# Second cross attention of a decoder on one core: scores in 64-row passes, three of four maxima copied and merged in one operation

## What is computed

```
x = stable_layernorm(x, g_norm)
q = x @ Wq;  k, v = split(context @ Wkv)            # 8 heads of 64
k, v = concat(null_kv, k), concat(null_kv, v)       # one key more
q = l2norm(q) * q_scale;  k = l2norm(k) * k_scale
sim = q @ k.T * 8;  sim = where(mask, sim, -max)
attn = softmax(sim, axis=-1)                        # float32
out = stable_layernorm((attn @ v) @ Wo, g_out)
```

## Time and profile before

| | before |
|---|---|
| median of 3 runs | 2707.45 us (2706.44 to 2709.51) |
| span of the profiled execution, first to last instruction | 2706.5 us |
| PE busy | 2391.5 us (88%) |
| DVE busy | 2051.9 us (76%) |
| ACT busy | 1528.1 us (56%) |
| mean granted TensorE clock, as a share of full speed | 0.929 |
| exponentials of the stage, line 2490 | 408, 433.1 us |
| adds, line 2802 | 400, 486.8 us |
| takes, line 2740 | 208, in three forms by source |
| merges, line 2751 | 192, 127.4 us |

### The profile page before, as it was taken

One profiled execution on the slowest core, in us unless ns is written; L12 is line 12 of the kernel. 1 busy time (PEld: TensorE's weight loads), 2 busy tenths in 40 slices (PEclk: granted clock), 3 DMA queues, 4 the chain that ended last, 5 costly groups with the idle time before them and its releaser, 6 DMA issues. The chain is left out here.

```text
span 2706.5 us, 33877 instructions
## 1 busy us (share of the span) xinstructions
PE 2391.5 (88%) x10276; PEld 872.1 (32%) x10276; DVE 2051.9 (76%) x3028; ACT 1528.1 (56%) x1858; POOL 302.4 (11%) x333
## 2 busy tenths in 40 slices
PE   6888677999999979998466599999999999997998
PEld 3555411222222224444122133323333333332443
DVE  5676698999995224344797888989999998976775
ACT  5555496777768843333443566666666666653111
POOL 5665500000000000000164100000000000000000
PEclk8898957999999989999698599999999999998998
DMA  5454471220001159954003331122113111111100
GB/s 142 134 166 140 132 109 35 62 66 27 26 24 29 31 111 215 212 152 117 17 0 65 77 96 30 29 64 71 30 30 105 30 30 29 31 36 69 47 0 8
DMA packets 198858, 191.06 MB, mean 71 GB/s; under 512 B 18288, under 2 KB 159125, under 8 KB 197905
## 3 DMA queue, kind: packets, MB, share of 16 engines
q1 hardware_dynamic: 198573, 189.13, 27.0%
q10 hardware_dynamic: 144, 0.10, 0.0%
HBM read 144.28 MB, written 41.42 MB: 69 GB/s over the span
## 5 line engine op out<-in xcount | busy, mean ns | idle before, releaser
L2802 DVE TENSOR_TENSOR y_acc<-y_acc,y_probs 128x1024 f32<-128x1024 f32 x400 | 486.8, 1217 | 35.1 <-ACT y_probs L2490 23.3
L2490 ACT ACTIVATE y_probs<-y_E,y_mask_bias 128x1024 f32<-128x1024 f32 x408 | 433.1, 1111 | 72.0 <-PE y_E L2582 63.9
L1223 ACT ACTIVATE x_probs<-x_E 128x1024 f32<-128x1024 f32 x408 | 396.6, 1022 | 136.2 <-PE x_E L1283 134.2
L1406 DVE TENSOR_REDUCE x_maxima<-x_M 128x1 f32<-128x496 f32 x660 | 410.5, 669 | 27.4 <-PE x_M L1265 17.1
L2591 PE MATMUL y_O<-y_probs,y_values 128*64 128x512 f32 x1632 | 400.1, 611 | 0.0
L2581 PE MATMUL y_E<-y_qa,y_ks 128*128 128x512 f16 x816 | 313.4, 384 | 1.5 <-ACT y_copied L2463 1.2
L2582 PE MATMUL y_E<-y_qb,y_ks 66*128 66x512 f16 x816 | 311.6, 382 | 0.0
L2463 ACT ACTIVATE y_copied<-y_M 128x1024 bf16<-128x1024 f32 (+1 forms) x164 | 162.4, 990 | 213.1 <-PE y_M L2545 213.1
L2740 DVE TENSOR_REDUCE y_maxima<-y_M 128x2 f32<-128x1024 f32 (+2 forms) x195 | 231.2, 1186 | 41.2 <-PE y_M L2545 31.4
L1874 DVE TENSOR_TENSOR f_hidden<-f_act_out,f_spread 128x512 f32<-128x512 f32 x160 | 110.7, 693 | 174.2 <-ACT f_act_out L1705 143.2
L1296 PE MATMUL x_O<-x_probs,x_values 128*32 128x512 f32 x1632 | 218.1, 606 | 0.4 <-ACT x_probs L1223 0.4
(11 more groups left out here) (503 smaller groups left out, 3159.1 us busy)
## 6 DMA issues: line engine op xcount, KB each, us to landing
f_spread<-comb_dram SPq DMA_DIRECT2D x160, 256.0 KB, 5.9
y_values<-v_dram SPq DMA_DIRECT2D x208, 128.0 KB, 2.2
v_dram<-a_v_out SPq DMA_DIRECT2D x26, 512.0 KB, 2.6
k_dram<-a_k_parts SPq DMA_DIRECT2D x26, 512.0 KB, 3.3
x_values<-v_dram SPq DMA_DIRECT2D x100, 128.0 KB, 2.2
f_weights<-f_w_in SPq DMA_DIRECT2D x40, 256.0 KB, 8.8
y_ks<-k_dram SPq DMA_DIRECT2D x75, 128.0 KB, 2.8
v_dram<-a_v_out SPq DMA_DIRECT2D x26, 256.0 KB, 2.1
```

The costliest lines, as they stand in the source:

```text
L1223: nc.scalar.activation(probs[:, n % 2, 2 * g:2 * g + 2, :], psE[:, 2 * g:2 * g + 2, :], ACT.Exp).then_inc(exped, 1)
L1406: V.tensor_reduce(maxima[:, 2 * h + j, qt, c:c + 1], psM[(2 * entry + j) % 3][:, 0:CHUNK0], AX.X, ALU.max).then_inc(max_done, 1)
L2490: A(probs[:, i, :], psE[:, 2 * (i % 2):2 * (i % 2) + 2, :].rearrange("p a b -> p (a b)"), ACT.Exp, bias=mask_bias[:, bass.ds(c * TILES_IN_ ...
L2802: ins = V.tensor_tensor(acc[:, u % 2, :], acc[:, u % 2, :], probs[:, i, :], ALU.add)
```

## The change

The second fp16 arrangement goes: keys and queries are no longer stacked by parts, and head j keeps rows 64 j to 64 j + 63 in one tile each (`keys`, `q_parts`). The scores of a tile are now four pairs of 64-row matmuls, the two heads of a pair side by side in the array: high on high, low on high, high on low, and a pair that adds the maxima (`m_ones` on `m_rows`). The DMAs that laid out `qa` and `qb` are gone, and the key loads take 2 DMAs instead of 5.

Of the four maxima of a chunk DVE takes only the first. ACT copies the other three, and one DVE operation merges all three (128x3072). All four maxima of the main part use `psM`, one after the other. On PE a half turn is now: a maximum, the scores of two tiles, a maximum, `weigh` of two tiles. Cut to its core:

```diff
-        copied = sb("copied", [P, 2, 2 * 512], BF16)
+        copied = sb("copied", [P, 3, 2, 512], BF16)
-        PV0, MAX0, SUM0, SPARE0, MERGED0 = 4, 2, 4, 2, 2
+        PV0, MAX0, SUM0, SPARE0, MERGED0 = 4, 2, 4, 3, 2
+        def spare_number(u, c, q):
+            return c * SPARES + (SPARES * KEY_TURNS * u + q - 1)
+        def merge_number(u, c):
+            return c + ((KEY_TURNS - 1) * u - 1)
...
# ACT
-                def copy_spare(u, c, g, scores=psM[:]):
+                def copy_spare(u, c, q, scores=psM[:]):
...
-                        e.wait_ge(S["merged"], merge_number(u, c, g) + 1)
-                        out = copied[:, g, :].rearrange("p (j n) -> p j n", j=2)
+                        e.wait_ge(S["merged"], merge_number(u, c) + MERGED0)
+                        out = copied[:, q - 1, :, :]
...
-                            if i == 1 and not (u == 0 and isinstance(c, int) and c == 0):
-                                copy_spare(*before(u, c), 1)
-                            if i == 3:
-                                copy_spare(*ahead(u, c), 0)
+                            if i == 0 and not (u == 0 and isinstance(c, int) and c == 0):
+                                copy_spare(*before(u, c), 3)
+                            if i >= 2:
+                                copy_spare(*ahead(u, c), i - 1)
# PE
+                def next_maximum(u, c, q):
+                    if q != 1:
+                        e.wait_ge(S["spare_copied"], spare_number(u, c, max(q, 1)) + SPARE0)
+                    if q < 2:
+                        e.wait_ge(S["max_done"], number(u, c) + (q + MAX0))
+                    maximum(u, c, q, psM, S["spare_mm"] if q else S["max_mm"])
...
+                    for key_part, q_part in ((0, 0), (1, 0), (0, 1)):
+                        for j in range(2):
+                            r = head_rows(j)
+                            T.matmul(psE[:, 2 * slot + j, :], keys[r, u // 2 % 2, key_part, tile * P:tile * P + P],
+                                     q_parts[r, q_part, u // 2, q0:q0 + HALF], start=(key_part + q_part == 0), stop=False)
...
+                            next_maximum(*ahead(u, c), 2 * g)
                                 for i in range(2):
                                     scores(u, c * TILES_IN_TURN + (2 * g + 2 + i), i, n + (2 + i))
-                            late_first(*ahead(u, c), g)
+                            next_maximum(*ahead(u, c), 2 * g + 1)
...
-                            late_spare(*ahead(u, c), g)
# DVE
-                    e.wait_ge(S["spare_copied"], number(u, c, g) + 1 + SPARE0)
-                    e.wait_ge(S["merged"], merge_number(u, c, g) - 1 + MERGED0)
+                    e.wait_ge(S["spare_copied"], spare_number(u, c, 3) + 1 + SPARE0)
+                    e.wait_ge(S["merged"], merge_number(u, c) + MERGED0)
...
-                            if i == 0 and not (u == 0 and at == 0):
-                                merge(*before(u, c), 1)
+                            if i == 0:
+                                take(*ahead(u, c))
+                            if i == 1 and not (u == 0 and at == 0):
+                                merge(*before(u, c))
...
-                            if i == 2:
-                                merge(*ahead(u, c), 0)
-                            if i % 2 == 0:
-                                take(*ahead(u, c), i // 2)
```

More of the change, by code:

```diff
@@ L2343, in load_keys @@
                     for part in range(2):
[L2344 to L2350, removed]
-                load_keys(0, 0, KVP)
[L2353 to L2369, removed]
+                        sp.dma_start(keys[:, slot, part, bass.ds(at, n)], d.k1_dram[:, part, pair, bass.ds(at, n)])\
+                            .then_inc(k_loaded[slot], 16)
+                load_keys(0, 0, KVP)
                 for u in range(UNITS):
@@ L2373, in _ @@
                     sp.wait_ge(S["m_row"], u + 1)
-                    for part in range(M_PARTS):
-                        sp.dma_start(qb[DH1 + part:DH1 + part + 1, u, :, :],
-                                     mrow[8 * part:8 * part + 8, :]).then_inc(S["m_placed"], 16)
+                    for j in range(2):
+                        sp.dma_start(m_rows[DH1 * j:DH1 * j + M_PARTS, u % 2, :],
+                                     mrow[4 * M_PARTS * j:4 * M_PARTS * (j + 1), :]).then_inc(S["m_placed"], 16)
                     def load_values(c):
@@ L2832, in finish @@
                         step(ins)
-                e.wait_ge(S["consts"], 3)
-                for g in range(2):
-                    take(0, 0, g)
+                e.wait_ge(S["consts"], 4)
+                take(0, 0)
                 with e.Fori(1, LAST) as c:
-                    for g in range(2):
-                        take(0, c, g)
-                        merge(0, c, g)
-                for g in range(2):
-                    take(0, LAST, g)
-                    merge(0, LAST, g)
+                    take(0, c)
+                    merge(0, c)
+                take(0, LAST)
+                merge(0, LAST)
                 for part in range(4):
@@ L2846, in _ @@
                 for c in range(LEAD):
-                    for g in range(2):
-                        take(1, c, g)
-                        merge(1, c, g)
+                    take(1, c)
+                    merge(1, c)
                 for u in range(UNITS):
@@ L3248, in layout @@
     a["x1_qs"], a["x1_ks"] = w["L1_xattn_q_scale"], w["L1_xattn_k_scale"]
-    a["x1_ones"] = np.ones((M_PARTS, 2 * KVP), np.float16)
+    a["x1_ones"] = np.zeros((P, P), np.float16)
+    for j in range(2):
+        a["x1_ones"][DH1 * j:DH1 * j + M_PARTS] = 1
     a["x1_g"], a["x1_gout"] = w["L1_xattn_g_norm"], w["L1_xattn_g_out"]
```

177 lines of the change are left out of this document (85 added, 92 removed).

## The result

| | before | after |
|---|---|---|
| median | 2706.94 us (2702.03 to 2709.51, 4 runs) | 2761.93 us (2759.33 to 2771.36, 4 runs) |
| ratio | | 1.0203, 95% interval 1.0183 to 1.0224 |
| span of the profiled execution | 2706.5 us | 2769.6 us (2771.36 as device time, the longest of its four) |

A forecast was written before the change was run, and what follows sets the result against it. PE bounded the kernel before, DVE close behind; after the change, a ring of waits at 9.8 us a turn. Terms of 14.6 + 5.1 + 26.2 + 7.1 - 0.5 = +52.5 gave 2760 us, range 2736 to 2812.

The forecast's parts named there:

- The ring: In a turn, copy, PE's matmuls, take, add 1, merge and next copy wait in a circle: 9.8 us, not 8.3.
- The full-engine reading: Rival theory from the experiments: engines are too full for the new work; half the merge would stay at 2762 us.
- the list: One turn's predicted starts from its first copy: fourth maximum 3.06, take 5.68, add 1 6.81, merge 8.01, next copy 9.82.
- PE's saving: In each half turn on PE, two changes of arrangement fewer at 0.1 us each: 4.16 us instead of 4.36.
- The units: Main part: a unit takes 123.3 us against 117.4; unit 0 +5.1, units 1 to 5 +26.2, unit 6 +7.1.
- The turns without a tie: Turns in a unit that wait for no merge: 6.9 us with narrow copies, 8.3 with nothing to merge.
- The one with the transpose: The turn in a unit with the transpose of the maxima on PE: 10.1 us.
- Unit 7: Unit without maxima: same changes of arrangement, score pairs cheaper in all, -0.5 us.
- The stretch ahead of unit 0: Before unit 0, three copies and a merge one after the other, 4.83 us a chunk; PE starts 1.6 earlier: +14.6 us.
- The sum: All terms, 14.6 + 5.1 + 26.2 + 7.1 - 0.5 = +52.5 us, giving 2760 us.
- The clock: Rival: PE falls to 1.2 GHz behind waits of about 1.5 us in tied turns; +50, 2810 us, chance 0.17.
- The rule on PSUM: Skill's warning that tiling does not speed up emptying PSUM; by it alone, ACT at 7.5, a turn stays PE's 8.3 us.

The follow-up runs named there:

- moving it by 1.13: The kernel after, with DVE's merge placed before the second add of the turn instead of behind it: 2686.65 us, 0.9924 of before.
- opening the ring: The kernel after with a second set of the three copies, so a copy waits for the merge of the chunk before the last: 2649.5 us, 0.9789 of before.
- the wait alone: The kernel before with one number changed, so a copy waits for all earlier merges instead of all but the latest: 2709.14 us, 1.0003 of before.
- half a merge: The kernel after, with the merge leaving out the second half of each copy's columns: 2694.9 us, 0.9971 of before.
- the score passes alone: The kernel before with only the change's 64-row scores and their layout; two takes, copies and merges in the old order: 2674.23 us, 0.9881 of before.

## Why the prediction was right

**The ring** was the step that decided, and it held: 9.81 against 9.82. Shortening one member by 0.80 or moving it by 1.13 gave back just that in every turn; opening the ring gave PE's pace; the wait alone gave nothing. The full-engine reading, by which half a merge would have changed nothing, is out.

That it held to 0.01 is in part luck. The take started 0.54 behind its maximum, not 0.43, and an add of 1.13 for 1.20 and PE's start 0.04 earlier made up for it. And the list left out the way that ended last: third maximum and scores, on PE, which reach the fourth maximum at 3.03 where the way listed, over ACT's second copy, gave 3.06. Had the two not lain so close, the turn would have been off by the difference. The copies waited 75 times, where the bounds were worked out for some 60 turns: 0.3 us on each would have been 23 us either way, not 18.

**PE's saving**: half turn 4.14 for 4.16, a unit 109.2 with the ring open. It was real all along, and in after it became idle time. The Trainium skill, TensorEngine Tiling (Array Packing), "Key Properties", says that changing the tiling mode drains TensorE. The trace agrees, with 0.22 us for two changes fewer. By that rule alone this change is a gain, as the run with the score passes alone is.

**The units.** Measured against predicted: unit 0 120.8 for 121.7, units 1 to 5 617.5 for 616.5, unit 6 118.8 for 118.7. Together +38.6 for +38.4. The turns without a tie at the end of a walk: 7.0 for 6.9 (the one with narrow copies), 8.3 for 8.3 (nothing to merge). The one with the transpose took 10.65 for 10.1, and others were shorter: two of the seven plain ones 9.70 (the rest 9.81), chunk 12's 9.16 and the last 9.12, where 9.3 was said for each. So a unit's sum, 123.44 for 123.3, is right with errors of up to half a microsecond that cancel. Unit 7 was given -0.5, and from its first add to the end of its weighing it took 95.81 for 95.87, so -0.1.

**The stretch ahead of unit 0** is the term that was mis-sized: +12.1 for +14.6. The 2 x 0.98 + 1.02 for three copies was too long, since two copies in a row take 1.94: a chunk took 4.68, not 4.83, which over 11 chunks is 1.7 of the 2.5 us; the other 0.8 was not followed. The start without a DMA wait came 1.6 us earlier as predicted.

**The sum**: in the stage's two pieces +50.8, where the terms for them make +53.0; behind them about nothing for -0.5; +55.0 by the medians for +52.5, and 2761.9 us for 2760. So the forecast was 2 us too high for the pieces that the change touches, and 2 us too low for the total. The 4 us between +50.8 and +55.0 are in no piece that the change touches; the four runs of after spread over 12 us, those of before over 7, and that leaves it open.

**The clock** was given 0.17 and did not fall. Behind 75 waits of 1.3 us on average, the longest 1.9, the granted clock of the unit windows is 1.00, so PE stayed at 2.4 GHz there. (The prediction set a duration, 3.40, against 1.87 from start to start; from start to start the slow weighing of the earlier trace rows took 3.33, which changes no term.)

**The rule on PSUM.** The Trainium skill, TensorEngine Tiling (Array Packing), "PSUM Bottleneck", says that with tiling the copies out of PSUM may become the bottleneck. ACT is busy for 90.2 and DVE for 102.1 of 124 us in a unit of after. Neither is full, so the trace does not agree for this kernel. For the score passes alone it agrees in the first turns of a unit, where PE waits for DVE.

## What to carry to other kernels

Before engine sums, count the places of every buffer that two engines share, find the instruction that frees one, and see what stands ahead of it on its engine; then follow one turn from start to start until it comes back to its first instruction. If that way is longer than the fullest engine's sum, it is the pace, and work saved on the full engine is worth nothing. The cures are one place more, the freeing instruction sooner, or smaller pieces that each free their own place: a merged operation that is cheaper to run can be dearer to wait for. And where two ways meet ahead of one instruction, time both: here they ended 0.04 us apart, and the one left out was the longer.

## What was not expected of the hardware

- The granted clock stayed at 1.00 behind 75 idle times of PE of 1.3 us on average, up to 1.9, with full work on both sides. Before, 1.62 us and a transpose of 128 columns stand at six unit ends; half clock followed at three of them, as in the earlier trace rows, and not at the other three, and with the score passes alone 1.73 us was followed by it at two of six. In after PE has no idle time before the transposes at the unit ends, and there is no half clock in units 0 to 6. So the length of an idle time alone does not tell what follows it here; what does was not tried.
- Two copies of 128x1024 from PSUM in a row on ACT take 1.94 us in all, where each has a duration of 1.02: the second starts 0.92 behind the first. A sum of durations is too long by 0.1 for each pair.
- The bf16 merge is linear in its length: 0.69 us for 1024 elements a partition, 0.95 for 1536, 1.75 for 3072.
